# A two-block transformer part on one core: keyed sum with query and key side by side, routed weights held by TensorE, one more shared group in front

## The chip, the cores and the metric

The kernel runs on one core of one Trainium2 chip, in one launch. The metric is the device time in microseconds (us) from the start to the end of an execution; lower is better. The engines of the core are PE (TensorE), DVE (VectorE), ACT (ScalarE), POOL (GpSimd) and SP (which only issues DMAs). Each runs a program of its own and waits on semaphores for the others.

## The reference

The input is x, 2048 tokens of D = 256 features in float32, and two blocks follow. Each is `x + a(norm(x))`, `ffn`, `x + b(norm(x))`, `ffn` with its own a, b and ffn. Three functions matter here. The keyed sum (the second mixer of the first block) sees the tokens as 2 sequences of 1024:

```python
QKV = jnp.einsum('bsd,ed->bse', X, W_in) + b_in
Q, K, V = jnp.split(QKV, 3, axis=-1)
Q = rope(Q, rot_dim)
K = rope(K, rot_dim)
A = jnp.sum(feature_map(K) * V, axis=-2)
Y = A[:, None, :] * Q
Y = jnp.einsum('bsd,ed->bse', Y, W_out) + b_out
```

rot_dim is 128, with interleaved pairs; feature_map(x) is x over the larger of its norm and 1e-12; the mixer also adds its own input to Y.

The first block's ffn, once after each mixer, with 4 experts and the one best for each token:

```python
g = jnp.einsum('td,edf->tef', x, Wg)
u = jnp.einsum('td,edf->tef', x, Wu)
h = jax.nn.silu(g) * u
y = jnp.einsum('tef,efd->ted', h, Wd)
```

Each goes from 256 to 1024 features and back; only the chosen expert's row is kept, times its probability.

The second block's ffn has 8 experts of 176 hidden features, the two best for each token, and a shared expert of 352 hidden features that every token passes.

## The kernel before

The 2048 tokens lie in SBUF as NT = 16 tiles of 128 (c.x), in NG = 4 groups of 4; a sequence of the keyed sum has BT = 8 tiles, FT = 2 is the count of 128-feature halves. Every stage is a class with one method for each engine (tensor, scalar, vector, gpsimd, sync), and Core lets each engine run its methods of all stages in a row, so an engine's order of work is the order of these calls; only semaphores tie the engines together. A float32 matmul is two passes of PE and shows as two records. The stages are: attention; routed ffn (profile time about 570 to 800 us); keyed sum and its projection (828 to 920); routed ffn (to 1162); linear attention; top-two ffn (1269 to 1471); attention; top-two ffn (1805 to the end).

**Routed (L1461 to L1640).** After the tokens are sorted by expert (choose, find_starts, place_tokens, set_rows, find_owners of Routing), the stage works on 19 tiles of 128 sorted rows, each of one expert. For tile k POOL gathers its rows from DRAM (gather, L1430) and PE turns them (turn_y, L1533; the copy back is set_y on DVE). `up(k)` (L1542) multiplies them with the expert's gate and up weights, four groups of 512 columns; the tokens are the stationary operand and the weights move, at an address made from the tile's owner, which is loaded into a register (tile_owner, L1458). ACT makes silu of the gate banks (L1597), DVE multiplies with the up banks (L1630). `turn_h(k)` (L1552) transposes the result in 8 blocks, ACT copies one half back (L1602) and DVE the other (L1635). `down(k)` (L1563) multiplies with the third weight matrix, ACT evicts (out, L1592), POOL scatters to DRAM (L1434). PE's order in a step is up(k), turn_y(k + 1), down(k - 1), turn_h(k). The steps between the first and the last run in a hardware loop (Fori).

**TopTwo (L1642 to L1943).** The same with 8 experts and 39 tiles, and a shared expert for all tokens in 4 groups of 512 tokens. A group is 3 steps n: shared_up(n) (L1752) and shared_down(n) (L1763), with shared_silu on ACT, shared_mul (L1889) and shared_add (L1896) on DVE. Group 0 stands ahead of the 39 tiles, between the steps of the sort; the groups 1 to 3 stand behind them (shared_steps). Behind them too, DVE adds the routed results to x in 8 pairs of tiles (L1448) with the next norm's steps (L280 to L291); `pairs_behind` says behind which step n each pair stands.

**KeyedSum (L1946 to L2107) and Project (L347 to L433).** For each of 16 tiles PE makes q, k and v (L2022; k and v in one bank, q in another). DVE adds the bias from PSUM in three operations (L2066, L2067, L2071), and multiplies the first 128 features of q and k by cos (L2081, one each) and by sin (L2083, two each, for the interleaved pairs). POOL adds the two parts (L1992, one for q, one for k), ACT squares k and sums it (L2043), POOL takes the root of 8 tiles at once (L1997), DVE the reciprocal (L2054, L2056). `product(b)` on DVE (L2059) multiplies k by its norm's reciprocal and by v, 8 operations; it stands behind tile 9 for the first sequence and behind the loop for the second. Then PE sums over the tokens with a column of ones as the moving operand (L2031), for both sequences behind all products; DVE scales W_out by the sum (L2092); POOL adds the normed rows to x, a tile at a time in the loop (L2001, `xy`), and the bias of the projection, 16 operations behind its last root (L2009). Project turns q in 4 groups (L380), multiplies it with the scaled weights (L394), and DVE adds the result to x (L424) with the next norm, a pair of tiles at a time. `finished(pe, 0)` lets the projection start when all is rotated, and `finished(pe, 3)` waits for all scaled weights.

## Time and profile before

| | us |
|---|---|
| three runs, median (lowest to highest) | 2004.8 (2002.64 to 2005.82) |
| the profiled execution, own time | 2006.96 |
| its span, first to last instruction | 2005.2 |
| mean granted clock of TensorE, share of full speed | 0.935 |

Busy time in the span: PE 1801.9 us (90%), DVE 1121.3 (56%), ACT 755.6 (38%), POOL 555.1 (28%). PE's busy time counts matmuls alone; weight loads (1012.1 us) overlap them. A busy count includes the tail of a group of instructions, which overlaps the next group; distances between starts tell the pace. The row "x16" of a timeline is 16 instructions in a row of one line and shape. The share of a whole span says little of a stage: the stages have different limits, and each is read from its own stretch.

### The profile page before, as it was taken

The page shows a single profiled execution, that of the slowest core. Times are in us where ns is not written, and L with a number is a line of the kernel's source. Part 1 is how long each engine was busy: PE and PEld are TensorE (multiplying, and loading weights), DVE is VectorE, ACT ScalarE, POOL GpSimd, SP SyncE. Part 2 cuts the span into 40 slices and gives each one's busy share as a digit, 9 for nine tenths or more (in the row PEclk, how much of TensorE's full clock was granted, in tenths as well). Part 3 has the DMA queues.
Part 4 walks back from the last instruction along what each step waited for, and adds up shares of the span by engine and source line. Part 5 has one row for each costly group of instructions (what it writes and reads, how often), then busy time and mean ns, then how long its engine had stood idle before and what let it go on. Part 6 is the DMA issues. An engine that isn't in the chain of part 4 may idle for free.

```text
span 2005.2 us, 31961 instructions
## 1 busy us (share of the span) xinstructions
PE 1801.9 (90%) x10672; PEld 1012.1 (50%) x10673; DVE 1121.3 (56%) x2299; ACT 755.6 (38%) x1469; POOL 555.1 (28%) x954
## 2 busy tenths in 40 slices
PE   7799999999969999676999969888987999988888
PEld 4344444443346665354666636566553444455654
DVE  6688888887242221765222255733465888746334
ACT  3277777777421111112112111222132676752220
POOL 2322222222111111452111140266133222223650
PEclk9699999999689999778999989899996999998999
DMA  3311111113310000301000050122414122002223
GB/s 107 87 36 42 42 42 42 40 37 144 117 52 26 21 24 19 97 1 50 23 21 24 21 176 10 61 87 87 123 52 86 23 42 40 3 18 70 90 76 124
DMA packets 82074, 114.36 MB, mean 57 GB/s; under 512 B 17273, under 2 KB 61465, under 8 KB 81177
## 3 DMA queue, kind: packets, MB, share of 16 engines
q1 hardware_dynamic: 70808, 82.23, 14.4%
q0 software_dynamic: 11136, 30.42, 4.8%
...
## 4 chain that ended last, share of the span: by engine, by line
PE 70%; DVE 16%; issue 4%; DMA 3%; another core or an unknown queue 2%; POOL 1%; ACT 1%; SPq 0%; POOLq 0%; DVEq 0%; ACTq 0%
PE psum L1542 13%; PE psum L1064 9%; PE psum L1048 7%; DVE region_a L812 7%; PE psum L1563 7%; PE psum L1009 6%; PE psum L1781 4%; PE psum L1752 3%; PE psum L1763 2%; PE psum L1800 2%; PE psum L1552 2%; PE psum L1801 1%; PE psum L938 1%; PE psum L1033 1%
## 5 line engine op out<-in xcount | busy, mean ns | idle before, releaser
L812 DVE TENSOR_REDUCE region_a<-psum 128x1 f32<-128x640 f32 (+7 forms) x576 | 528.4, 954 | 109.1 <-PE psum L1014 57.6
L916 ACT ACTIVATE region_w<-psum 128x512 f32<-128x512 f32 x864 | 465.6, 600 | 222.7 <-PE psum L1048 219.3
L1542 PE MATMUL psum<-region_w,region_a 128*128 x608 | 271.2, 599 | 1.5 <-DVE region_a L1623 1.2
L1064 PE MATMUL psum<-region_w,region_a 128*32 128x512 f32 (+3 forms) x2304 | 253.8, 514 | 1.0 <-POOL region_w L739 0.6
L739 POOL TENSOR_SCALAR_AFFINE_SELECT region_w<-region_w 128x512 f32<-128x512 f32 x192 | 122.3, 637 | 458.7 <-ACT region_w L916 454.6
L1009 PE MATMUL psum<-region_a,y_norm 48*128 48x512 bf16 (+7 forms) x816 | 224.1, 351 | 4.9 <-DVE region_a L812 3.8
L1048 PE MATMUL psum<-y_norm,region_a 51*128 51x512 bf16 (+1 forms) x612 | 205.4, 399 | 7.0 <-DMA y_norm<-region_a 5.2
L1542 PEld LDWEIGHTS psum<-region_w,region_a 128*128 128x128 f32 x608 | 114.0, 193 | 132.2 <-issue 132.2
L1630 DVE TENSOR_TENSOR region_a<-psum,region_a 128x512 f32<-128x512 f32 x76 | 52.6, 692 | 215.1 <-PE psum L1542 215.1
L1430 POOL DMA_INDIRECT region_a<-token_rows,region_a x116 | 113.1, 975 | 147.5 <-DVE region_a L1406 86.8
L1563 PE MATMUL psum<-region_w,region_a 128*128 x608 | 137.7, 379 | 1.9 <-ACT region_a L1602 1.9
L1434 POOL DMA_INDIRECT answer_rows<-region_a x38 | 37.6, 990 | 345.5 <-ACT region_a L1592 345.5
L1048 PEld LDWEIGHTS psum<-y_norm,region_a 51*128 51x128 bf16 (+1 forms) x612 | 51.0, 96 | 161.6 <-ACT region_w L916 108.6
L1563 PEld LDWEIGHTS psum<-region_w,region_a 128*128 128x128 f32 x608 | 112.7, 190 | 17.1 <-issue 3.3
L1597 ACT ACTIVATE region_a<-psum 128x512 f32<-128x512 f32 x76 | 45.4, 597 | 187.3 <-PE psum L1542 187.3
L1012 PE MATMUL psum<-region_a 64*128 64x128 bf16 x512 | 112.5, 226 | 0.0
L1781 PE MATMUL psum<-region_w,region_a 128*128 x312 | 111.5, 482 | 0.3 <-DVE region_a L1901 0.2
L1635 DVE COPY region_a<-psum 128x512 f32<-128x512 f32 x38 | 26.3, 692 | 127.9 <-PE psum L1552 127.9
L1014 PE MATMUL psum<-region_a,identb 64*128 64x64 bf16 x512 | 97.8, 193 | 0.0
L1434 POOL DMA_INDIRECT answer_rows<-ctx,region_a x78 | 77.2, 990 | 66.8 <-ACT ctx L1861 49.1
L323 PE MATMUL psum<-identf,y_norm 128*128 128x128 f32 x256 | 44.7, 326 | 52.4 <-DVE y_norm L291 42.2
L1752 PE MATMUL psum<-y_t,region_w 128*128 128x512 f32 (+1 forms) x192 | 85.7, 594 | 0.9 <-ACT ctx L1861 0.9
...
## 6 DMA issues: line engine op xcount, KB each, us to landing
...
```

The costliest lines, as they stand in the source:

```text
L739: pool.affine_select(p, p, pattern=[[0, GQ], [1, P]], channel_multiplier=-1, base=0, compare_op=ALU.is_ge, fill=0.0)\
L812: dve.tensor_reduce(dst, src, AX_X, ALU.max, negate=True).then_inc(self.ring_done.sem, 1)
L916: act.activation(self.p[col % P_RING][:, :, i % 4, :], c.bank[ST_BANKS[s % 3]].rearrange("p (h t) -> p h t", h=GQ), ACT.Exp, scale=self.sc ...
L1009: mm = pe.matmul(bank[:, 0:n], q, kp[lo_row:hi_row, lo:lo + n], start=True, stop=not diag, skip_group_check=True)
L1048: mm = pe.matmul(bank[:, :], self.kp[slot][0:self.srows, P * j:P * j + P], self.qp[slot][0:self.srows, :, P * i:P * i + P], start=True, st ...
L1064: mm = pe.matmul(c.bank[ACC_BANK][32 * h:32 * h + 32, P * lo:512], self.vp[slot][:, j, :], self.p[col % P_RING][:, h, lo:4, :], start=(j = ...
L1430: pool.indirect_dma_start(y, None, self.c.tokens[:, :], bass.IndirectOffsetOnAxis(ap=self.row_in[:, k:k + 1], axis=0)).then_inc(done.sem, 16)
L1434: pool.indirect_dma_start(self.c.answers[0:self.spare_rows + self.top * NTOK, :], bass.IndirectOffsetOnAxis(ap=self.row_out[:, k:k + 1], a ...
L1542: mm = pe.matmul(bank[:, :], self.yt[:, f, :], w[:, f, bass.ds(own * self.hidden + 512 * half, 512)], start=(f == 0), stop=(f == FT - 1))
L1563: mm = pe.matmul(c.bank[7][:, 0:D], self.ht[:, j, :], self.wd[:, bass.ds((own * (last + 1) + j) * D, D)], start=(j == 0), stop=(j == last))
L1752: mm = pe.matmul(c.bank[6 * (n % 2) + k][0:m, :], weight[:, f, P * j:P * j + m], c.yt[:, f, 512 * g:512 * g + 512], start=(f == 0), stop=( ...
L1781: mm = pe.matmul(self.gu_bank[j][:, 0:2 * self.hidden], self.yt[j][:, f, :], w.wgu[:, f, bass.ds(owner[k] * (2 * self.hidden), 2 * self.hi ...
```

## The change

Three stages are edited.

- KeyedSum: q and k lie side by side in one buffer `qk`. PE makes q|k first (512 columns), then v (256), and each is waited for by itself. DVE adds one bias to q|k, takes cos and sin for q and k together (1 and 2 operations), and multiplies k by v, without the norm, two tiles later. POOL rotates q and k in one operation and adds the projection's bias in the loop. PE's sum takes the norm's reciprocal of each token as its moving column, in place of ones. The first sequence's sum stands behind tile 13, the second's inside the projection, ahead of its third turn. The reciprocals and the scaling of weights move with them, by `before_pair` and `finished`.
- Routed: per tile ACT copies the expert's gate weights and DVE its up weights into one of two buffers, and PE holds 128x128 blocks of these while the turned tokens move, so that h comes out transposed. turn_h and both copies of it are gone. h is double buffered, the loops are unrolled.
- TopTwo: shared group 1 stands in front of the tiles; behind them stand groups 2 and 3, with `pairs_behind` fitted to it.

Long runs of removed lines stand in the functions above.

```diff
-            own = self.tile_owner(pe, k)
             pe.wait_ge(self.y_set.sem, self.y_set.at(k + 1))
             for half in range(2):
...
+                if k:
+                    pe.wait_ge(self.h_done.sem, self.h_done.at(2 * k - 1 + half))
+                for w, copied, bank, done in ((self.gate[k % 2], self.gate_copied, c.bank[half], self.gprod),
+                                              (self.upper[k % 2], self.up_copied, c.bank[2 + half], self.uprod)):
+                    if half == 0:
+                        pe.wait_ge(copied.sem, copied.at(k + 1))
+                    for q in range(4):
+                        for f in range(FT):
+                            mm = pe.matmul(bank[:, P * q:P * q + P],
+                                           w[:, f, 512 * half + P * q:512 * half + P * q + P],
+                                           self.yt[:, f, :], start=(f == 0), stop=(f == FT - 1))
                     mm.then_inc(done.sem, 1)
 
...
+        def down(k):
+            own = owner.pop(k)
+            pe.wait_ge(self.h_done.sem, self.h_done.at(2 * k + 2))
+            if k:
                 pe.wait_ge(self.o_set.sem, self.o_set.at(k))
             last = self.hidden // P - 1
             for j in range(last + 1):
-                mm = pe.matmul(c.bank[7][:, 0:D], self.ht[:, j, :], self.wd[:, bass.ds((own * (last + 1) + j) * D, D)],
-                               start=(j == 0), stop=(j == last))
+                mm = pe.matmul(c.bank[7][:, 0:D], self.h[k % 2][:, j, :],
+                               self.wd[:, bass.ds((own * (last + 1) + j) * D, D)], start=(j == 0), stop=(j == last))
             mm.then_inc(self.down.sem, 1)
 
-        def step(k, first, last):
+        turn_y(0)
+        owner[0] = self.tile_owner(pe, 0)
+        for k in range(self.tiles):
             up(k)
-            if not last:
+            if k + 1 < self.tiles:
                 turn_y(k + 1)
...
+                owner[k + 1] = self.tile_owner(pe, k + 1)
+            if k:
+                down(k - 1)
+        down(self.tiles - 1)
...
-        def step(k, first, last):
+        def copy_gate(k):
+            own = self.tile_owner(act, k)
+            if k >= 2:
+                act.wait_ge(self.gprod.sem, self.gprod.at(2 * k - 2))
+            act.activation(self.gate[k % 2], self.wg[:, :, bass.ds(own * self.hidden, self.hidden)], ACT.Copy)\
+                .then_inc(self.gate_copied.sem, 1)
+
+        self.weights.wait(act)
+        act.wait_ge(self.owners.sem, self.owners.at(1))
+        self.places_read(act)
+        for k in range(2):
+            copy_gate(k)
+        for k in range(self.tiles):
+            if k >= 1 and k + 1 < self.tiles:
+                copy_gate(k + 1)
             for half in range(2):
                 act.wait_ge(self.gprod.sem, self.gprod.at(2 * k + half + 1))
+                if k:
+                    act.wait_ge(self.h_done.sem, self.h_done.at(2 * k - 1 + half))
                 act.activation(self.g[:, 512 * half:512 * half + 512], c.bank[half][:, :], ACT.Silu)\
                     .then_inc(self.silu.sem, 1)
...
+            if k:
+                out(k - 1)
...
+        def copy_up(k):
+            own = self.tile_owner(dve, k)
+            if k >= 2:
+                dve.wait_ge(self.uprod.sem, self.uprod.at(2 * k - 2))
+            dve.tensor_copy(self.upper[k % 2], self.wu[:, :, bass.ds(own * self.hidden, self.hidden)])\
+                .then_inc(self.up_copied.sem, 1)
+
+        self.weights.wait(dve)
+        dve.wait_ge(self.owners.sem, self.owners.at(1))
+        self.places_read(dve)
+        set_y(0)
+        for k in range(2):
+            copy_up(k)
+        for k in range(self.tiles):
+            if k >= 1 and k + 1 < self.tiles:
+                copy_up(k + 1)
+            h = self.h[k % 2].rearrange("p j t -> p (j t)")
             for half in range(2):
                 at = slice(512 * half, 512 * half + 512)
                 dve.wait_ge(self.uprod.sem, self.uprod.at(2 * k + half + 1))
                 dve.wait_ge(self.silu.sem, self.silu.at(2 * k + half + 1))
-                dve.tensor_tensor(self.h[:, at], c.bank[2 + half][:, :], self.g[:, at], ALU.mult)\
+                if k >= 2:
+                    dve.wait_ge(self.down.sem, self.down.at(k - 1))
+                dve.tensor_tensor(h[:, at], c.bank[2 + half][:, :], self.g[:, at], ALU.mult)\
                     .then_inc(self.h_done.sem, 1)
-            if not last:
+            if k + 1 < self.tiles:
                 set_y(k + 1)
...
+        shared_up(3)
         self.invert(pe, 1)
         shared_down(2)
+        shared_up(4)
+        shared_down(3)
+        shared_up(5)
+        shared_down(4)
+        shared_down(5)
         pe.wait_ge(self.owners.sem, self.owners.at(1))
-        pe.wait_ge(self.s_added.sem, self.s_added.at(2))
+        pe.wait_ge(self.s_added.sem, self.s_added.at(4))
         for k in range(2):
             turn_y(k)
             owner[k] = self.tile_owner(pe, k)
@@ -1832,7 +1850,7 @@
         self.every_tile(step)
         down(self.tiles - 1)
         pe.wait_ge(self.o_set.sem, self.o_set.at(self.tiles))
-        self.shared_steps(pe, (1, 2, 3), shared_up, shared_down, {8: 0})
+        self.shared_steps(pe, (2, 3), shared_up, shared_down, {10: 0})
...
         shared_add(0)
+        for n in range(3, 6):
+            shared_mul(n)
+        shared_add(1)
         dve.wait_ge(self.h_clear.sem, self.h_clear.at(RING))
         for k in range(2):
             set_y(k)
         mul(0)
         self.every_tile(step)
-        pairs_behind = {5: 0, 6: 1, 7: 2, 8: 3, 10: 4, 11: 5}
-        for n in range(3, 3 * NG):
+        pairs_behind = {7: 0, 8: 1, 9: 2, 10: 3, 11: 4}
+        for n in range(6, 3 * NG):
             shared_mul(n)
-            if n % 3 == 1 and n > 4:
+            if n % 3 == 1 and n > 7:
                 shared_add(n // 3 - 1)
             if n in pairs_behind:
                 self.next_norm.pair(dve, pairs_behind[n])
         shared_add(NG - 1)
-        self.next_norm.pair(dve, 6)
-        self.next_norm.pair(dve, 7)
+        for n in range(5, NT // 2):
+            self.next_norm.pair(dve, n)
...
         def rotated(t):
 
-            pool.wait_ge(self.cosm, 2 * t + 2)
-            pool.wait_ge(self.sinm, 4 * t + 4)
-            for n, z in enumerate((c.cx[:, D * t:D * t + P], self.k[:, t, 0:P])):
-                pool.tensor_tensor(z, self.ta[t % 2][:, n, :], self.tb[t % 2][:, n, :], ALU.add).then_inc(self.rot, 1)
+            pool.wait_ge(self.cosm, t + 1)
+            pool.wait_ge(self.sinm, 2 * t + 2)
+            pool.tensor_tensor(self.qk[:, t, :, 0:P], self.ta[t % 2], self.tb[t % 2], ALU.add).then_inc(self.rot, 1)
 
         def root(b):
             s = slice(b * BT, b * BT + BT)
@@ -2003,10 +2024,21 @@
                 rotated(t - 1)
             if t == BT + 1:
                 root(0)
+            pool.wait_ge(self.xy, t + 1)
+            pool.tensor_tensor(c.x[:, t, :], c.x[:, t, :], self.bias_out, ALU.add).then_inc(self.biased, 1)
         rotated(NT - 1)
         root(1)
-        for t in range(NT):
-            pool.tensor_tensor(c.x[:, t, :], c.x[:, t, :], self.bias_out, ALU.add).then_inc(self.biased, 1)
+
+    def sum_up(self, pe, b):
+
+        c = self.c
+        pe.wait_ge(self.kv, (b + 1) * BT)
+        pe.wait_ge(self.norm_step, 2 * b + 2)
+        for f in range(FT):
+            for t in range(b * BT, b * BT + BT):
+                mm = pe.matmul(c.bank[7][:, f:f + 1], c.yn[:, t, P * f:P * f + P], self.rnorm[:, t:t + 1],
+                               start=(t == b * BT), stop=(t == b * BT + BT - 1))
+        mm.then_inc(self.sums, 1)
...
-                if t >= 2:
-                    pe.wait_ge(self.lin, 2 * (t - 1))
-                    pe.wait_ge(self.v_done, t - 1)
-                for bank, lo, n in ((2 * (t % 2), D, 2 * D), (2 * (t % 2) + 1, 0, D)):
+                for i, (lo, n, free) in enumerate(((0, 2 * D, self.lin), (2 * D, D, self.v_done))):
+                    if t >= 2:
+                        pe.wait_ge(free, t - 1)
                     for f in range(FT):
...
+                        mm = pe.matmul(c.bank[2 * (t % 2) + i][:, 0:n], c.yt[:, f, P * t:P * t + P],
+                                       self.w[:, f, lo:lo + n], start=(f == 0), stop=(f == FT - 1))
+                    mm.then_inc(self.prod, 1)
+                if t == BT + 5:
+                    self.sum_up(pe, 0)
...
+    def invert_norm(self, dve, b):
+        s = slice(b * BT, b * BT + BT)
+        dve.wait_ge(self.root, b + 1)
+        dve.tensor_scalar(self.norm[:, s], self.norm[:, s], 1e-12, None, ALU.max).then_inc(self.norm_step, 1)
+        dve.wait_ge(self.norm_step, 2 * b + 1)
+        dve.reciprocal(self.rnorm[:, s], self.norm[:, s]).then_inc(self.norm_step, 1)
+
+    def scale_weights(self, dve, b):
+        dve.wait_ge(self.sums, b + 1)
+        for f in range(FT):
+            dve.tensor_scalar(self.ws[b][:, f, :], self.wo[:, f, :], self.c.bank[7][:, f:f + 1], None,
+                              ALU.mult).then_inc(self.scaled, 1)
...
+        def key_value(t):
+            dve.wait_ge(self.rot, t + 1)
+            dve.wait_ge(self.v_done, t + 1)
+            dve.tensor_tensor(c.yn[:, t, :], c.yn[:, t, :], self.qk[:, t, 1, :], ALU.mult).then_inc(self.kv, 1)
 
         for t in range(NT):
-            kv, q = c.bank[2 * (t % 2)], c.bank[2 * (t % 2) + 1]
+            qk, v = c.bank[2 * (t % 2)], c.bank[2 * (t % 2) + 1]
             bt = t % BT
-            dve.wait_ge(self.prod, t + 1)
-            dve.tensor_tensor(cx[:, t, :], q[:, 0:D], self.bias[:, 0:D], ALU.add).then_inc(self.lin, 1)
-            dve.tensor_tensor(self.k[:, t, :], kv[:, 0:D], self.bias[:, D:2 * D], ALU.add).then_inc(self.lin, 1)
-
+            dve.wait_ge(self.prod, 2 * t + 1)
+            dve.tensor_tensor(self.qk[:, t, :, :].rearrange("p n d -> p (n d)"), qk[:, :], self.bias[:, 0:2 * D],
+                              ALU.add).then_inc(self.lin, 1)
+
+            dve.wait_ge(self.prod, 2 * t + 2)
             dve.wait_ge(self.xy, t + 1)
             self.ln.ready(dve, t // 4)
-            dve.tensor_tensor(c.yn[:, t, :], kv[:, D:2 * D], self.bias[:, 2 * D:3 * D], ALU.add).then_inc(self.v_done, 1)
-
-            dve.wait_ge(self.lin, 2 * t + 2)
+            dve.tensor_tensor(c.yn[:, t, :], v[:, 0:D], self.bias[:, 2 * D:3 * D], ALU.add).then_inc(self.v_done, 1)
+
+            dve.wait_ge(self.lin, t + 1)
             if t >= 2:
-                dve.wait_ge(self.rot, 2 * t - 2)
-            a, b = self.ta[t % 2], self.tb[t % 2]
+                dve.wait_ge(self.rot, t - 1)
+            a, b, z = self.ta[t % 2], self.tb[t % 2], self.qk[:, t, :, 0:P]
             sin = self.sin[:, bt, :].rearrange("p (n e) -> p n e", e=2)
...
+            dve.tensor_tensor(a, z, over(self.cos[:, bt, :], 1, 2), ALU.mult).then_inc(self.cosm, 1)
+            pair, bp = (y.rearrange("p m (n e) -> p m n e", e=2) for y in (z, b))
+            for e in range(2):
+                dve.tensor_tensor(bp[:, :, :, e], pair[:, :, :, 1 - e], over(sin[:, :, e], 1, 2), ALU.mult)\
+                    .then_inc(self.sinm, 1)
+            if t >= 2:
+                key_value(t - 2)
+            if t == BT + 3:
+                self.invert_norm(dve, 0)
+        key_value(NT - 2)
+        key_value(NT - 1)
+        self.scale_weights(dve, 0)
+
+    def before_pair(self, dve, n):
+        if n == 0:
+            self.invert_norm(dve, 1)
+            dve.wait_ge(self.biased, NT)
+        if n == 2:
+            self.scale_weights(dve, 1)
 
     def source(self, t, f):
-        return self.c.cx[:, D * t + P * f:D * t + P * f + P]
+        return self.qk[:, t, 0, P * f:P * f + P]
 
     def out_weights(self, t, f):
         return self.ws[t // BT][:, f, :]
 
     def finished(self, pe, g):
-        if g == 0:
-            pe.wait_ge(self.rot, 2 * NT)
+        pe.wait_ge(self.rot, 4 * g + 4)
+        if g == 1:
+            pe.wait_ge(self.scaled, FT)
+        if g == 2:
+            pe.wait_ge(self.project.ot1, (NG - 1) * self.project.k + 1)
+            self.sum_up(pe, 1)
+        if g == 3:
             pe.wait_ge(self.scaled, NB * FT)
```

## Rows read from the trace of the kernel before

**Rows 1.** The page's part 4: the chain that ended last, by engine.

```profile
PE 70%; DVE 16%; issue 4%; DMA 3%; another core or an unknown queue 2%; POOL 1%; ACT 1%; SPq 0%; POOLq 0%; DVEq 0%; ACTq 0%
```

**Rows 2.** Table by stretches: first routed and keyed-sum stage; busy us (instructions).

```profile
578.90:799.90 221.00, 219.63 (x796) 135.14 (x796) 45.42 (x75) 40.52 (x76) 35.07 (x36) 0.99 0.07 21
827.80:920.20 92.40, 76.61 (x314) 55.73 (x312) 68.80 (x234) 15.71 (x46) 48.04 (x84) 0.87 0.01 2
```

**Rows 3.** Timeline of PE, one routed tile: start, us, line, operands, count.

```profile
669.65 7.03 PE L1542 MATMUL psum<-region_w,region_a 128*128 x16
...
676.74 3.62 PE L1563 MATMUL psum<-region_w,region_a 128*128 x16
680.20 1.04 PE L1552 MATMUL psum<-identf,region_a 128*128 128x128 f32 x8
681.07 7.03 PE L1542 MATMUL psum<-region_w,region_a 128*128 x16
```

**Rows 4.** Timeline of PE, linear attention: 129-column passes with own weights.

```profile
1225.79 7.31 PE L2211 MATMUL psum<-region_w,region_a 128*128 128x129 f32 x64
```

**Rows 5.** Timeline of PE, the keyed sum's two sums by a one-column matmul.

```profile
874.80 3.63 PE L2031 MATMUL psum<-region_a 128*128 128x1 f32 x32
888.06 6.99 PE L2031 MATMUL psum<-region_a 128*128 128x1 f32 x32 [9.63 <-DVE region_a L2059]
```

**Rows 6.** Timeline of PE, the end of the first routed stage.

```profile
796.13 3.71 PE L1563 MATMUL psum<-region_w,region_a 128*128 x16 [0.95 <-ACT region_a L1602]
```

**Rows 7.** Groups of instructions by shape: evictions of the routed stages; busy, mean ns.

```profile
L1630 DVE TENSOR_TENSOR region_a<-psum,region_a 128x512 f32<-128x512 f32 x76 | 52.6, 692 | 215.1 <-PE psum L1542 215.1
...
L1597 ACT ACTIVATE region_a<-psum 128x512 f32<-128x512 f32 x76 | 45.4, 597 | 187.3 <-PE psum L1542 187.3
...
L1592 ACT ACTIVATE region_a<-psum 128x256 f32<-128x256 f32 x38 | 14.6, 384 | 183.9 <-PE psum L1563 183.9
```

**Rows 8.** Timeline of POOL in the same tile: gather of the next rows.

```profile
671.02 0.97 POOL L1430 DMA_INDIRECT region_a<-token_rows,region_a  x1 [0.30 <-issue]
```

**Rows 9.** Timeline of DVE in the keyed-sum loop, second half.

```profile
866.32 0.88 DVE L2083 TENSOR_TENSOR region_a<-ctx,region_a 128x64 f32<-128x64 f32 x2
...
868.79 0.88 DVE L2083 TENSOR_TENSOR region_a<-ctx,region_a 128x64 f32<-128x64 f32 x2
...
876.68 0.36 DVE L2083 TENSOR_TENSOR region_a<-region_a 128x64 f32<-128x64 f32 x2
```

**Rows 10.** Timeline of POOL beside it: the add of the normed rows (xy).

```profile
866.18 0.80 POOL L2001 TENSOR_TENSOR x_res<-x_res,y_norm 128x256 f32<-128x256 f32 x1
```

**Rows 11.** Timeline of DVE: the second half's products, then two pairs of the projection.

```profile
881.31 6.70 DVE L2059 SCALAR_TENSOR_TENSOR region_a<-region_a,y_norm 128x256 f32<-128x256 f32 x8
...
907.93 0.75 DVE L424 TENSOR_TENSOR x_res<-psum,x_res 128x256 f32<-128x256 f32 x2
...
910.09 0.75 DVE L424 TENSOR_TENSOR x_res<-psum,x_res 128x256 f32<-128x256 f32 x2
```

**Rows 12.** Timeline of PE: two steps of the shared expert behind the tiles.

```profile
1424.70 1.89 PE L1763 MATMUL psum<-region_w,ctx 128*128 128x256 f32 x8
...
1429.86 1.89 PE L1763 MATMUL psum<-region_w,ctx 128*128 128x256 f32 x8
```

**Rows 13.** Timeline of DVE behind the last shared add: two pairs with their norm.

```profile
1463.13 0.87 DVE L1448 SCALAR_TENSOR_TENSOR x_res<-y_norm,region_a,x_res 128x256 f32<-128x256 f32 x2
...
1466.20 0.88 DVE L1448 SCALAR_TENSOR_TENSOR x_res<-y_norm,region_a,x_res 128x256 f32<-128x256 f32 x2
```

**Rows 14.** Timeline of PE ahead of the first top-two tiles.

```profile
1287.74 0.39 PE L1396 MATMUL psum<-region_a 128*128 128x117 bf16 x4 [1.80 <-DVE region_a L1379]
...
1295.07 1.47 PE L1774 MATMUL psum<-identf,region_a 128*128 128x128 f32 x4 [1.43 <-DVE x_res L1896]
1296.64 2.71 PE L1781 MATMUL psum<-region_w,region_a 128*128 x4
...
1301.27 1.35 PE L1781 MATMUL psum<-region_w,region_a 128*128 x4
```

143 lines of the change are left out of this document (32 added, 111 removed).

## The prediction

> **What bounds the kernel now.** I read the chain of work that ended last first: TensorE (PE) carries 70% of it, VectorE (DVE) 16% [rows 1]. So most of the change is judged by PE's time. The table by stretches then shows the two kinds of stage that it touches: in a routed stage PE is busy for 219.63 of 221.00 us at a granted clock of 0.99, so nothing but fewer PE microseconds helps there; in the keyed-sum stage PE is busy for 76.61 of 92.40 us and DVE for 68.80, at 0.87, so there the order of the steps decides [rows 2]. Last come the timelines of single engines for the terms of the sum. Run-to-run differences here allow about 0.2% (4 us) to be told from no change.
>
> **Routed stages (two, 19 tiles each).** One tile is 11.42 us, from one start of L1542 to the next (681.07 - 669.65). L1542 takes 6.86 of it as 16 passes of 512 columns (0.429 each), with turn_y (0.22) to L1563's start at 676.74; down (L1563) takes 3.46 to 680.20; the turns of h (L1552, 8 passes) take 0.87 [rows 3]. The change makes the up step 32 matmuls, so 64 passes of 128 columns, each with its own weight load, and drops the turns. The nearest row is another stage's: 64 passes of 129 columns with weights of their own in 7.31 us, so 0.1117 apart (7.31 less the last pass's tail, 64 ways) [rows 4]. A second row agrees: 32 passes of one column in 3.63 [rows 5]; the price is the weight load and not the columns. Up becomes 64 x 0.1117 = 7.15, 0.29 more; the turns give 0.87 back. The static addresses and the single expert load a tile change only what PE's queue issues, and 1.4 us in 221 is all the idleness there is, so I count nothing. New tile: 7.15 + 0.22 + 3.45 = 10.82, 0.60 less; for 17 intervals 10.2 us.
> At the stage's end PE now turns h (1.0), waits 0.95 for the copy of it and does the last down [rows 6]; turns and wait both go, 2.0. Against it, down(18) must wait for out(17) to free the only bank, about 0.65 by the 0.38 of such an eviction [rows 7] and a hand-over. At the start the first passes run at the lower clock, where 128-column passes cost no more than the four times longer ones relative to full speed: nothing. Per stage 10.2 + 2.0 - 0.65 = 11.5, twice is 23.0.
> What must stay covered: ScalarE (ACT) copies 2048 columns of gate weights a tile, DVE as many up weights. By the 512-column eviction, 0.597 (ACT) and 0.692 (DVE) [rows 7], four such are 2.4 and 2.8; by the slope between the 256- and 512-column evictions ACT needs 1.9. Either lies in a tile in which each engine has over 6 us free (45 us of DVE and 41 of ACT work in 221, of which the h copies go) [rows 2]. POOL issues the row gather at 671.02, 1.4 us after L1542 started [rows 8]; the up step that hides it and its landing gets no shorter. If a copy delayed a tile, the price would be the delay past some 2 us of slack, 38 times. Bounds for the two stages together: 17 (each tile 0.15 dearer) to 26.
> The Trainium skill ("SBUF — State Buffer", the warning box "The 'DVE blocks DMA' trap (SWDGE)") speaks against this part: an fp32 SBUF-to-SBUF copy on DVE locks GpSimd out of the shared port, so that it can't write a gather's descriptors. If it did so for the whole copy each tile, the gather would come 2 to 3 us later, within about 2 us of slack: at worst 1 us a tile, 38 us in all. Copy and gather stand in no row together here.
>
> **Keyed sum and its projection.** PE needs 4 passes each of 512 and 256 columns a tile, 4 x 0.429 x 1.5 = 2.57 us [rows 3]. DVE's tile lasts 2.47 in the second half, from one L2083 pair of 0.88 to the next (868.79 - 866.32), of which 0.52 is a wait for POOL's add at 866.18 (0.80), since the last pair, without one, takes 0.36; so 1.95 [rows 9, 10]. The new tile has one 512-column add for two of 256, two sine products for four and one product k*v of 256 columns: about 2.0 alone. POOL now does its rotation as one operation and the bias add (L2009) inside the loop, so three of DVE's operations meet POOL's. Bounds of a tile: 2.58, where PE sets it, and 3.45, where each SBUF operation of DVE waits for one of POOL's 0.80; I take 2.8, since one wait of 0.52 a tile is the rule now [rows 9] and I expect one to two. Reading starts earlier by 1.5, as DVE waits for 8 passes of half clock and not 12 (first copy at 831.3). 16 x 2.8 = 44.8 from there, plus 1 for sum_up(0), which holds PE for 3.6, and 0.8 for the reciprocal gives 877 to 878; two products and two scalings of 0.3 more, 880.
> Before, the tail after the loop (877.04) was: root and reciprocal to 881.31, eight products 6.70, PE's second sum at the lower clock 6.99 from 888.06 after an idle 9.63, then scaling and turns before the first product [rows 5, 11]. Now the norm rides as the moving column, so the 6.70 stands in the loop; and sum_up(1) comes inside the projection, while PE is warm. New: turn(1) waits for the scaled weights, 880 to 881; multiply(0) to 884.7; sum_up(1) 3.6 to 888.3 (32 passes at 0.1117 [rows 5]); turn(2) and multiply(1) to 892.7, whose first pair is read at about 891.2; six pairs at 2.16 (910.09 - 907.93) [rows 11] follow, ending at about 905 with the last norm against 920.2 [rows 2]. invert_norm(1) and its wait for the bias adds stand in DVE ahead of pair 0: behind them are queued all adds of the projection, so root(1) on POOL (1.65) is hidden only because multiply(0) takes 3.5. **Saved: 15.2**, by the tile's bounds 8 to 18.
>
> **Front groups of the top-two stages.** A step of a shared group (up and down) takes 5.16, from one down to the next (1429.86 - 1424.70) [rows 12], so a group is 3 x 5.16 = 15.5 of PE. Moving one to the front takes 15.5 from behind, but one more pair (5, 6, 7, not 6, 7) now follows the last add: 3.07 with norm (1466.20 - 1463.13) [rows 13], so the back of the first such stage saves 12.4; in the last stage a pair is only its two L1448 groups, 1.6, and the gain 13.9. In front PE idles 1.8 us before the second inversion and 1.4 before turn_y(0) [rows 14]; the new steps fill only the first, since turn_y still waits for an add. turn_y(0) comes at about 1305.6 for 1295.07, 10.6 later: 15.5 less the hole filled, less 3 us of DVE's work on rows and owners that now runs under PE's steps. The third product of group 1 is queued on DVE behind that work and shared_add(0), so down(3) may wait some 0.5; I leave that in the bounds. After it L1781's first four passes took 2.71 [rows 14], twice the 1.35 of those from 1301.27 on; with PE kept busy ahead the clock is up already, and of the 4 us between 2.0 come back. Front cost 8.6; net 3.8 and 5.3, together 9.0. Bounds 5 (no clock gain) to 13 (the inversion's wait goes whole).
>
> **The sum.** 23.0 + 15.2 + 9.0 = 47.2 us. The profiled execution lasted 2006.96 us, so 1959.8; it stood 2.2 above the median of the runs, 2004.8, so **1958** on the median.
>
> **Rivals.** (A) DVE and POOL alternate in every operation of the keyed-sum loop: 3.45 a tile, 16 x 0.65 = 10.4 more, 1968. For it: L2059 beside POOL's adds took 0.84 each (6.70 for 8) [rows 11], as long as an add of POOL. Against: only one pair of four meets one in rows 9. The Trainium skill ("SBUF — State Buffer", section "SBUF: two separate sides") states that one of the pair takes the port for the whole instruction and the other fully blocks; by that every meeting costs up to 0.8, and it leans to A. By that the trace agrees: 0.52 was lost under an add that ran on for 0.66 [rows 9, 10].
> (B) The front groups don't fill holes and the clock doesn't rise earlier: 5 us less gain, 1962 to 1963.
> (C) The other side, **slower**: the 128-column passes with own weights run at the lower clock. [rows 5] hold both levels for weight-bound passes: 32 in 3.63 at 2.4 GHz and 32 in 6.99 at 1.2 GHz. The up step would be 64 x 0.214 = 13.7, 6.5 more than with the clock up; over 38 tiles 247 us, so 2205, and 2300 if turn_y and down are slowed with it (3.67 more a tile, less what overlaps). Its turning point: the other parts save 24.2, the tiles 0.60 x 38 = 22.8; over 64 x 38 = 2432 passes 47.0 is 0.019, so from a mean pass of 0.131 on the kernel is slower. Against it: the 64 passes of 129 columns in rows 4 ran at full speed and followed a full-clock stretch; for it: they lasted only 7 us, and no row shows such a mix for 200 us.
> (D) It doesn't do what it says: the copies or the gather come late, 1 us a tile, 38 less, 1996.
>
> **Chances.** Forecast (1950 to 1964, with B in it) 0.61; A 0.18; better than it, up to 1945, 0.05; D 0.07, a seventh of it near no change; C 0.04 and slower by something not seen here 0.03; no change from several small losses 0.02. The range, 1943 to 1982, holds forecast, A and half of D. Faster by over 0.2%: 0.61 + 0.18 + 0.05 + 0.06 = 0.90; within it 0.01 + 0.02 = 0.03; slower 0.07.
>
> **What would show it.** L1542's successor as x64 in about 7.3 us and a period of 10.8 with no idle before it; no L1552; granted clock 0.99 in the routed stretches. DVE's tile in the keyed sum at 2.8, and the projection's pairs ending near 905 after the earlier shift of 11.5. sum_up(1) in 3.6 and not 7. L1781's first four passes in 1.4 after turn_y(0). Wrong would be: idle before turn_y or before up in each tile (D), passes of 0.2 (C), a POOL add under every DVE operation (A), a first pair that waits for POOL's root.

## The result

The changed kernel took 1968.8 us (median of 4 runs, 1968.63 to 1969.58) against 2003.7 for the kernel before in the same rounds (4 runs, 2002.1 to 2005.82): a ratio of 0.9816, with a 95% interval of 0.9804 to 0.9829. The forecast was 1958. The profiled executions were 1968.63 and 2006.96 us, 38.3 apart where the sum said 47.2.

The profile after, first its busy times and the chain by engine (before: [rows 1]); PE is the bound as it was:

```profile
PE 1776.6 (90%) x12192; PEld 1134.3 (58%) x12192; DVE 1134.2 (58%) x2235; ACT 802.7 (41%) x1469; POOL 553.6 (28%) x937
...
PE 71%; DVE 15%; issue 4%; DMA 3%; another core or an unknown queue 2%; POOL 2%; ACT 1%; SPq 0%; POOLq 0%; DVEq 0%; ACTq 0%
```

The table by stretches (before: [rows 2]); the columns are stretch, its length, busy us and instructions of PE, PEld, DVE, ACT and POOL, granted clock, DMA share, GB/s. Both routed stages and the keyed sum:

```profile
581.80:791.40 209.60, 207.83 (x1556) 199.05 (x1556) 55.06 (x76) 61.66 (x75) 35.06 (x36) 0.99 0.07 24
819.40:901.70 82.30, 76.72 (x316) 53.59 (x317) 63.89 (x170) 15.45 (x46) 45.69 (x67) 0.91 0.01 2
921.90:1132.10 210.20, 208.52 (x1556) 199.68 (x1556) 54.98 (x75) 61.52 (x74) 35.01 (x36) 0.99 0.07 24
```

The first routed stage lasts 209.6 for 221.0, the keyed sum 82.3 for 92.4 to 92.8. PEld is nearly as busy as PE now in the routed stages (199.05 for 207.83 us, 135.14 before): each pass has its own weight load.

Where the time went, from PE's first instruction of each stretch to that of the next (us); a routed stretch ends with its last down, and the last stretch with DVE's last add. "Other traces" are those of the experiments below whose code in the stretch is that of the changed kernel (for a stretch that no edit touches, all of them):

| stretch | before | after | difference | other traces |
|---|---|---|---|---|
| start to the first router (no edit) | 559.57 | 562.42 | +2.85 | 557.7 to 565.7 |
| routed, first | 220.86 | 209.41 | -11.45 | 209.2 to 209.7 |
| keyed sum and projection | 92.79 | 82.30 | -10.49 | 79.0 to 83.4 |
| routed, second | 220.59 | 210.10 | -10.49 | 209.1 to 210.7 |
| top-two 1: front | 27.20 | 37.67 | +10.47 | 37.5 to 37.7 |
| top-two 1: tiles | 117.65 | 118.64 | +0.99 | 116.5 to 120.4 |
| top-two 1: behind | 57.38 | 44.98 | -12.40 | 44.98 to 44.99 |
| top-two 2: front | 27.33 | 37.53 | +10.20 | 37.5 |
| top-two 2: tiles | 117.47 | 114.04 | -3.43 | 115.3 to 121.2 |
| top-two 2: behind | 51.21 | 37.31 | -13.90 | 37.31 |
| all other stretches up to that add (no edit) | 509.85 | 509.14 | -0.71 | |

The routed tile in the trace after (PE; start, us, line, operands; before: [rows 3]), and the end of the stage (before: [rows 6]):

```profile
667.94 7.31 PE L1549 MATMUL psum<-region_a,ctx 128*128 128x128 f32 x64
675.09 0.38 PE L1533 MATMUL psum<-identf,region_a 128*128 128x128 f32 x2
675.30 3.62 PE L1561 MATMUL psum<-region_w,region_a 128*128 x16
678.76 5.41 PE L1549 MATMUL psum<-region_a,y_norm 128*128 128x128 f32 x47
```

```profile
783.27 3.62 PE L1561 MATMUL psum<-region_w,region_a 128*128 x16
787.57 3.72 PE L1561 MATMUL psum<-region_w,region_a 128*128 x16 [0.69 <-ACT region_a L1585]
```

678.76 - 667.94 is 10.82, and 16 of the stage's 18 intervals are 10.82; the first two are 10.23 and 10.92. The 64 passes take 7.31 as those of [rows 4] did. At the end the last down waits 0.69 for the eviction of the one before.

The weights' copies, on DVE and then on ACT, and what POOL issues in that tile (before: [rows 8]):

```profile
665.46 1.23 DVE L1629 COPY y_norm<-region_w 128x2048 f32 x1
```

```profile
668.79 1.91 ACT L1591 ACTIVATE y_norm<-region_w 128x2048 f32 x1 [0.27 <-issue]
```

```profile
668.80 0.99 POOL L1437 DMA_INDIRECT answer_rows<-region_a  x1 [8.55 <-ACT region_a L1585]
670.10 0.97 POOL L1433 DMA_INDIRECT region_a<-token_rows,region_a  x1 [0.30 <-issue]
```

DVE's 2048 columns take 1.23 us, not the 2.8 that I had from four PSUM evictions; ACT's take 1.91, as the slope said. DVE's copy is over at 666.7, POOL's first issue starts at 668.8: they never meet.

The keyed-sum loop on DVE, one tile of the second half (before: [rows 9]):

```profile
843.10 0.68 DVE L2096 TENSOR_TENSOR region_a<-psum,region_a 128x512 f32<-128x512 f32 x1
843.70 0.41 DVE L2102 TENSOR_TENSOR y_norm<-psum,region_a 128x256 f32<-128x256 f32 x1
844.03 0.70 DVE L2109 TENSOR_TENSOR region_a<-region_a,ctx 128x256 f32<-128x256 f32 x1
844.66 1.01 DVE L2112 TENSOR_TENSOR ctx<-region_a,ctx 128x128 f32<-128x128 f32 x2
845.59 0.41 DVE L2090 TENSOR_TENSOR y_norm<-y_norm,region_a 128x256 f32<-128x256 f32 x1
845.93 0.68 DVE L2096 TENSOR_TENSOR region_a<-psum,region_a 128x512 f32<-128x512 f32 x1
```

845.93 - 843.10 is 2.83. L2109 (cosines, 0.70) and L2112 (sines, 1.01 for two) each hold one wait for POOL, since they take 0.41 and 0.48 where POOL is idle. But the end of the loop and the start of the projection hold something that isn't in the forecast. PE's timeline there, and its granted clock (the first of the last three numbers of a row) in slices of 2 us:

```profile
858.99 4.26 PE L2039 MATMUL psum<-region_a,y_norm 128*128 128x1 f32 x32 [0.32 <-DVE region_a L2075]
863.11 8.21 PE L2053 MATMUL psum<-region_a,y_t 128*128 128x512 f32 x16
871.16 1.04 PE L382 MATMUL psum<-identf,region_a 128*128 128x128 f32 x8
874.74 1.12 PE L382 MATMUL psum<-identf,region_a 128*128 128x128 f32 x8 [2.54 <-DVE ctx L2080]
875.66 5.29 PE L396 MATMUL psum<-ctx,y_t 128*128 128x256 f32 x16
880.78 3.63 PE L2039 MATMUL psum<-region_a,y_norm 128*128 128x1 f32 x32
```

```profile
859.00:861.00 2.00, 2.00 (x19) 2.00 (x19) 2.00 (x7) 0.12 (x2) 1.17 (x3) 1.00 0.00 0
861.00:863.00 2.00, 2.00 (x16) 2.00 (x15) 2.00 (x4) 0.51 (x2) 2.00 (x3) 0.74 0.00 0
863.00:865.00 2.00, 2.00 (x5) 0.97 (x5) 0.80 (x3) 0.51 (x2) 1.50 (x3) 0.50 0.00 0
865.00:867.00 2.00, 2.00 (x4) 0.97 (x3) 0.09 (x1) 0.00 (x0) 0.75 (x2) 0.50 0.00 0
867.00:869.00 2.00, 2.00 (x5) 1.35 (x5) 0.98 (x3) 0.00 (x0) 0.00 (x0) 0.55 0.00 0
869.00:871.00 2.00, 2.00 (x8) 1.19 (x7) 1.61 (x6) 0.27 (x1) 1.07 (x2) 1.00 0.00 0
...
877.00:879.00 2.00, 2.00 (x6) 1.63 (x5) 0.42 (x1) 0.00 (x0) 0.00 (x0) 0.50 0.00 0
```

L2039 is the first sum, 32 passes of one column: it starts at the full clock, and 3 us into it the clock falls to 1.2 GHz, while PE is busy in 100% of the slice. The 16 passes behind it, the two last tiles of the loop, end at 871.3, 8.1 after the sum, where two tiles at full clock are 2 x 2.57; DVE waits for them. A second low stretch follows PE's 2.54 us of idle time at 872 to 874.7: multiply(0) (L396) takes 5.12 to the next start (880.78 - 875.66) where later ones take 3.45.

### The profile page after: what moved, and what is told of

Its sections match the earlier page's. It is cut to its first block, busy times and chain, and to the rows that moved or that the text cites. A ratio compares the mean times of both kernels' runs of the same rounds, so it can differ in the third digit from the quotient of the medians.

```text
span 1966.9 us, 34312 instructions
## 1 busy us (share of the span) xinstructions
PE 1776.6 (90%) x12192; PEld 1134.3 (58%) x12192; DVE 1134.2 (58%) x2235; ACT 802.7 (41%) x1469; POOL 553.6 (28%) x937
## 4 chain that ended last, share of the span: by engine, by line
PE 71%; DVE 15%; issue 4%; DMA 3%; another core or an unknown queue 2%; POOL 2%; ACT 1%; SPq 0%; POOLq 0%; DVEq 0%; ACTq 0%
PE psum L1549 14%; PE psum L1067 9%; PE psum L1051 8%; DVE region_a L815 7%; PE psum L1561 7%; PE psum L1012 6%; PE psum L1764 4%; PE psum L1793 4%; PE psum L1775 2%; PE psum L1812 2%; PE psum L1813 1%; PE psum L941 1%; PE psum L2240 1%; PE psum L1036 1%
## 5 line engine op out<-in xcount | busy, mean ns | idle before, releaser
L1012 PE MATMUL psum<-region_a,y_norm 48*128 48x512 bf16 (+7 forms) x816 | 228.2, 356 | 4.9 <-DVE region_a L815 4.2
L1549 PEld LDWEIGHTS psum<-region_a,ctx 128*128 128x128 f32 x1280 | 149.9, 196 | 3.0 <-DVE region_a L1623 2.0
L1549 PE MATMUL psum<-region_a,ctx 128*128 128x128 f32 x1280 | 150.4, 280 | 1.2 <-DVE region_a L1623 1.2
L1561 PE MATMUL psum<-region_w,region_a 128*128 x608 | 137.8, 380 | 1.4 <-ACT region_a L1585 1.4
L1549 PE MATMUL psum<-region_a,y_norm 128*128 128x128 f32 x1152 | 131.7, 275 | 1.8 <-DVE region_a L1623 1.8
L1549 PEld LDWEIGHTS psum<-region_a,y_norm 128*128 128x128 f32 x1152 | 131.3, 192 | 3.1 <-DVE region_a L1623 2.3
L1561 PEld LDWEIGHTS psum<-region_w,region_a 128*128 128x128 f32 x608 | 112.5, 190 | 16.0 <-issue 2.2
L1793 PE MATMUL psum<-region_w,region_a 128*128 x312 | 109.0, 473 | 0.7 <-issue 0.7
L1012 PEld LDWEIGHTS psum<-region_a,y_norm 48*128 48x128 bf16 (+1 forms) x816 | 66.2, 100 | 41.4 <-DVE region_a L815 21.3
```

The costliest lines, as they stand in the source:

```text
L1012: mm = pe.matmul(bank[:, 0:n], q, kp[lo_row:hi_row, lo:lo + n], start=True, stop=not diag, skip_group_check=True)
L1549: mm = pe.matmul(bank[:, P * q:P * q + P], w[:, f, 512 * half + P * q:512 * half + P * q + P], self.yt[:, f, :], start=(f == 0), stop=(f = ...
L1561: mm = pe.matmul(c.bank[7][:, 0:D], self.h[k % 2][:, j, :], self.wd[:, bass.ds((own * (last + 1) + j) * D, D)], start=(j == 0), stop=(j == ...
L1793: mm = pe.matmul(self.gu_bank[j][:, 0:2 * self.hidden], self.yt[j][:, f, :], w.wgu[:, f, bass.ds(owner[k] * (2 * self.hidden), 2 * self.hi ...
```

## The experiments

Each is timed against the kernel before in the same rounds. The chips differed (the kernel before had medians of 2011.4, 2008.7 and 2006.5 us on the three), so ratios are compared, or stretches of traces.

### One part alone, three times

The kernel before with the classes of one stage taken from the changed kernel: routed_only has Routed, keyed_only has KeyedSum with the hooks in Stage and Project, top_only has TopTwo.

> The kernel before with the edit of the routed stages alone. Theory: the edit's worth is the shorter tile, 10.82 us for 11.42, and the shorter end, 11.4 us a stage in the trace of the full change, so the time is about 22 us under the kernel before, ratio 0.989, and the first routed stage starts within 1 us of where it did (579.0). Rival, that the longer program (loops written out) costs elsewhere: the first routed stage starts 2.8 us later, as it did with all three edits, though no line ahead of it is changed; then the gain is 19 to 20.

> The kernel before with the edit of the keyed sum and its projection alone. Theory: it gives the 10.5 us that this stage gave within the full change, ratio 0.9948, and both falls of TensorE's granted clock show again: one in the 32 one-column passes of the sum inside the loop, one in the first product of the projection. Rival, that these falls were chance: one or both are missing, the stage takes 82.3 - 3.3 or - 1.7 us, and the gain is 12 to 15.

> The kernel before with the edit of the top-two stages alone. Theory: the backs save 12.4 and 13.9 us and the fronts cost 10.5 each, as in the full change, so 5 to 6 us net before what the clock does at the first tiles; with it (low there in the first stage and full in the second of the full change) 4 to 9, ratio 0.9955 to 0.998. Rival, that the forecast was right with 9.0: ratio 0.9955 with a full clock at the first tile of both stages.

Measured: routed_only 0.9928 (0.9906 to 0.9950), keyed_only 0.9939 (0.9915 to 0.9963), top_only 0.9952 (0.9935 to 0.9969). The three losses of time, 0.72, 0.61 and 0.48%, add to 1.81%; the whole change has 1.84%. So the parts are additive within what the timing resolves (0.17 to 0.24% each). routed_only's stages last 209.33 and 209.71; its first router starts at 558.25, earlier than in the kernel before, so the rival of a longer program that costs elsewhere is out: the +2.85 ahead of every edit is no part of the change (that stretch ran from 557.7 to 565.7 us in the traces shown here). The timed gain of routed_only, 15.6 us between the medians, is under the 22 that I expected, and the expected ratio of 0.989 lies outside the interval; its two stages have their 22.4, but the old keyed sum in that trace took 96.4 for 92.8 (after the 3.33 us in which PE waits for DVE's products, 32 passes took 13.33 for 10.56, so a low clock there), and the untouched tiles of the top-two stages took 120.2 and 121.8 for 117.6 and 117.5. keyed_only gave 9.4 us in its stretch (83.38) and shows both falls of the clock, and a third of 3.4 us further on. top_only has the fronts at 37.49 twice and the backs at 44.98 and 37.31.

### wide_sum and sum32: how many columns the sum moves

```diff
-                mm = pe.matmul(c.bank[7][:, f:f + 1], c.yn[:, t, P * f:P * f + P], self.rnorm[:, t:t + 1],
+                mm = pe.matmul(c.bank[7][:, P * f:P * f + P], c.yn[:, t, P * f:P * f + P],
+                               self.rnorm[:, t:t + 1].to_broadcast([P, P]),
...
-            dve.tensor_scalar(self.ws[b][:, f, :], self.wo[:, f, :], self.c.bank[7][:, f:f + 1], None,
+            dve.tensor_scalar(self.ws[b][:, f, :], self.wo[:, f, :], self.c.bank[7][:, P * f:P * f + 1], None,
```

sum32 is the same with 32 columns for 128.

> The changed kernel, but the sums' moving operand is the norm's reciprocal repeated over 128 columns, for 1 column; the results stand 128 times and one of them is read. Theory: a pass costs its weight load, 0.112 us, at 1 column as at 128, but with one column TensorE's granted clock falls during the sum in the loop (from 861.9 to 869.0) and costs 3.3 us; with 128 columns the clock stays up, the sum takes 3.6 for 4.3, the products behind it 2.57 a tile, and the kernel is 3.3 us faster than the changed kernel (about 1965.5). Rival, that the fall comes from the short idle times ahead of the sum (0.25 and 0.32 us) or by chance: it is there again and the time is 1968.8.

> The changed kernel with the reciprocal repeated over 32 columns as the sums' moving operand. [...]

PE in wide_sum, then its granted clock in the same stretch; below them PE in sum32:

```profile
856.90 3.81 PE L2039 MATMUL psum<-region_a,y_norm 128*128 128x128 f32 x32 [0.32 <-DVE region_a L2076]
860.54 5.32 PE L2054 MATMUL psum<-region_a,y_t 128*128 128x512 f32 x16
```

```profile
859.50:861.50 2.00, 2.00 (x14) 1.52 (x14) 2.00 (x5) 0.51 (x2) 1.51 (x2) 1.00 0.00 0
861.50:863.50 2.00, 2.00 (x8) 1.24 (x7) 1.06 (x3) 0.51 (x2) 2.00 (x3) 1.00 0.00 0
```

```profile
857.09 4.22 PE L2039 MATMUL psum<-region_a,y_norm 128*128 128x32 f32 x32 [0.32 <-DVE region_a L2076]
861.13 8.30 PE L2054 MATMUL psum<-region_a,y_t 128*128 128x512 f32 x16
```

With 128 columns the sum ends 3.64 after its start and the two tiles behind it take 5.17; the clock is 1.00 through both (the fall at multiply(0) stays: 5.10 to the next start). With 32 columns it is as with one: the sum 4.04, the tiles 8.1. From the sum's start to the loop's last pass:

| traces | columns | us |
|---|---|---|
| after, keyed_only, early_scale, late_copy, early_copy | 1 | 12.31 to 12.34 |
| no_bias_add | 1 | 12.24 |
| after_again, early_turn | 1 | 10.66, 10.67 |
| sum32 | 32 | 12.34 |
| wide_sum, all_four | 128 | 8.98, 8.97 |

All nine with 1 or 32 columns lose 1.7 or 3.4 us, none of the two with 128 does. In after_again and early_turn the fall begins later, behind the sum (6.93 for the two tiles), and their loops had come there 1.6 us earlier; so they lose less. The whole stage would not have shown the effect: 78.95 in wide_sum, 82.36 in sum32, but also 79.00 in after_again with one column, because there the clock rose 1.9 us after the stage's first pass, for 5.1 and 5.2 in wide_sum and sum32. The ratio of wide_sum, 0.9787 (0.9760 to 0.9815), isn't told apart from the changed kernel's 0.9816, nor the expected gain from the rival's none: 3.3 us is less than the other stretches vary.

### early_scale, early_copy: PE's wait ahead of the projection

early_scale moves the scaling of the first sequence's weights ahead of the last products; early_copy also moves the copies of the turned q ahead of DVE's last product and ACT's last square. The edit of early_copy, shortened; early_scale has only its lines with scale_weights:

```diff
             if t == BT + 3:
                 self.invert_norm(dve, 0)
+            if t == NT - 2:
+                self.scale_weights(dve, 0)
         key_value(NT - 2)
+        self.project.first_copy(dve)
         key_value(NT - 1)
-        self.scale_weights(dve, 0)
...
         for t in range(NT):
+            if t == NT - 1:
+                self.project.copy_turned(act, 0)
             act.wait_ge(self.rot, t + 1)
```

> The changed kernel with the scaling of the first sequence's weights moved on DVE from behind the loop's last two products to behind tile 14's steps, so that the projection's second turn finds it done. Theory: TensorE's 2.54 us of idle time ahead of that turn goes, and with it the fall of the granted clock from 875 to 879 that makes the first product 5.1 for 3.45: the keyed-sum stage takes 82.3 - 2.5 - 1.7, about 78.5 us by its stretch; the first fall, in the sum inside the loop, stays. Rival: the projection then waits for something else of the same length (the second reciprocal, whose root ends on POOL at 875.8, or the rotation), and the stage gains under 1 us.

> The changed kernel with the weights of the first sequence scaled behind tile 14, and the projection's first two copies of the turned q placed ahead of DVE's last product and ahead of ACT's last square. early_scale took away the wait for the scaled weights, and a wait for these copies of the same length came in its place (2.63 us). Theory: with both gone TensorE goes from its turns to the first product with under 1 us idle, the product takes 3.5 for 4.9, and the keyed-sum stage about 78.5 by its stretch. Rival: the second sum, which needs the root and the reciprocal of the second half (876.3 in the changed kernel's trace), waits instead and takes the gain back.

PE in early_scale, then in early_copy:

```profile
866.90 1.91 PE L382 MATMUL psum<-identf,region_a 128*128 128x128 f32 x16
871.44 5.23 PE L396 MATMUL psum<-ctx,y_t 128*128 128x256 f32 x16 [2.63 <-DVE y_t L420]
```

```profile
870.42 1.91 PE L382 MATMUL psum<-identf,region_a 128*128 128x128 f32 x16
874.39 5.38 PE L396 MATMUL psum<-ctx,y_t 128*128 128x256 f32 x16 [2.06 <-ACT y_t L418]
```

Both theories missed, and in early_scale the rival came true in kind: a wait of the same length, and 0.2 us gained. The second turn runs through (x16), but the wait comes back ahead of the first product, 2.63 and then 2.06 us, and the product behind it is slow as before (5.07 and 5.22 to the next start). The stretches are 82.06 and 81.94 for 82.30; the ratios 0.9812 (0.9793 to 0.9832) and 0.9805 (0.9780 to 0.9829). DVE works without a gap through the steps of tile 15 up to that copy (in early_copy from 868.15 to 873.57): it is DVE's queue that PE waits for. The row of early_copy names ACT, but ACT's copy for that product was over at 871.66; DVE's ended at 874.25, 0.14 before PE started, and in early_scale at 871.30, 0.14 before it too. What is left is to put the copy ahead of tile 15's own rotation; that wasn't tried.

### no_bias_add: one POOL operation fewer in each tile

The adds of the projection's bias on POOL and the wait for them are left out, so the output lacks that bias.

> The changed kernel without the adds of the projection's bias on POOL (left out altogether, so the output lacks that bias). Theory: the tile of 2.83 us in the keyed-sum loop is 2.58 of TensorE's own plus what DVE's sine and cosine steps wait for POOL; with two of POOL's operations a tile for three, one wait of 0.3 to 0.5 goes and the tile falls to TensorE's 2.58, so the stage gains 16 x 0.25 = 4 us. Rival, that the two-engine waits come from the rotation and the add of the normed rows alone: the tile stays at 2.8.

DVE, two starts of one line in the loop:

```profile
841.06 0.69 DVE L2094 TENSOR_TENSOR region_a<-psum,region_a 128x512 f32<-128x512 f32 x1 [0.22 <-PE psum L2051]
...
843.64 0.69 DVE L2094 TENSOR_TENSOR region_a<-psum,region_a 128x512 f32<-128x512 f32 x1 [0.22 <-PE psum L2051]
```

The tile is 2.58, PE's own pace, and the first sum starts 2.6 us earlier in the stage (37.0 for 39.6 after its first pass). So the waits for POOL that PE's pace doesn't hide were 0.25 of a tile. The stage took 81.29, only 1.0 less where 4 were expected: the first product took 4.6 to the next start, and a low clock in multiply(1) made it 5.14 for 3.45. The ratio is 0.9806 (0.9786 to 0.9826).

### late_copy: DVE's copy beside POOL's issue

```diff
             if k >= 1 and k + 1 < self.tiles:
+                if k >= 2:
+                    dve.wait_ge(self.o_set.sem, self.o_set.at(k - 1))
                 copy_up(k + 1)
```

> The changed kernel, but in the routed stages DVE starts its copy of 2048 columns only when the result of the tile before last is evicted, so that it runs at the same time as POOL's issue of the scatter (now 0.99 us) and ahead of the gather's. Theory from the trace of the change, where copy and issue never meet: there is some 2 us of slack, so the tile stays at 10.82 whatever the copy does to the issue. The rule of the Trainium skill (SBUF — State Buffer, the box on DVE blocking DMA) says that POOL can't write descriptors during the copy: the scatter's issue then takes 1.5 to 2.2 us for 0.99 and the gather's starts later by the same. Rival: they don't disturb each other, 0.99 and 0.97 as before.

POOL, then DVE:

```profile
664.57 1.86 POOL L1437 DMA_INDIRECT answer_rows<-region_a  x1 [7.69 <-ACT region_a L1585]
666.74 0.97 POOL L1433 DMA_INDIRECT region_a<-token_rows,region_a  x1 [0.30 <-issue]
```

```profile
665.08 1.23 DVE L1629 COPY y_norm<-region_w 128x2048 f32 x1 [3.83 <-ACT region_a L1585]
```

The scatter's issue takes 1.86 for 0.99 and ends 0.12 behind the copy. Of the 38 scatters 32 meet a copy: each takes 1.85 to 1.87 and ends 0.12 behind it, though it had started 0.5 us before it; the six that meet none take 0.97 to 0.99. The gather's own issue, behind it, stays at 0.97 and starts as much later. This agrees with the rule of the Trainium skill (SBUF — State Buffer, the box on DVE blocking DMA) that GpSimd can't write a DMA's descriptors while such a copy runs. It costs next to nothing here: of the intervals between tiles that are 10.82 in the trace after, one is 11.27 and the others stay, and the ratio is 0.9817 (0.9796 to 0.9839). The slack was there as forecast.

### early_turn: no wait for the add ahead of the tiles

```diff
+        turn_y(0)
+        owner[0] = self.tile_owner(pe, 0)
         shared_down(5)
-        pe.wait_ge(self.s_added.sem, self.s_added.at(4))
-        for k in range(2):
-            turn_y(k)
-            owner[k] = self.tile_owner(pe, k)
+        turn_y(1)
+        owner[1] = self.tile_owner(pe, 1)
         up(0)
```

The wait for the add stands ahead of turn_h(0), and DVE copies both turned tiles ahead of that add.

> The changed kernel, but in the top-two stages the turns of the first two routed tiles stand on TensorE ahead of and behind the last shared product of the front group, and the wait for the shared add stands ahead of the first use of its bank. Theory: the 3.2 us between the end of that product and the first routed product (1.43, 0.43 and 0.35 of them idle) fall to 0.5, the front takes about 34.8 for 37.5 in both stages, and the clock can't fall there: 5 us less in all. Rival: the rows' gather or DVE's copy is late instead and the front takes 37 or more.

First the changed kernel's two fronts (PE), then early_turn's first:

```profile
1270.97 3.62 PE L1775 MATMUL psum<-region_w,ctx 128*128 128x256 f32 x16
1276.02 0.41 PE L1786 MATMUL psum<-identf,region_a 128*128 128x128 f32 x2 [1.43 <-issue]
1276.85 0.43 PE L1786 MATMUL psum<-identf,region_a 128*128 128x128 f32 x2 [0.43 <-issue]
1277.64 2.01 PE L1793 MATMUL psum<-region_w,region_a 128*128 x4 [0.35 <-issue]
```

```profile
1810.72 0.41 PE L1786 MATMUL psum<-identf,region_a 128*128 128x128 f32 x2 [1.43 <-issue]
1811.38 0.43 PE L1786 MATMUL psum<-identf,region_a 128*128 128x128 f32 x2 [0.26 <-issue]
1812.19 1.45 PE L1793 MATMUL psum<-region_w,region_a 128*128 x4 [0.37 <-issue]
```

```profile
1267.72 0.38 PE L1786 MATMUL psum<-identf,region_a 128*128 128x128 f32 x2
1267.94 1.89 PE L1775 MATMUL psum<-region_w,ctx 96*128 96x256 f32 x8
1269.66 0.38 PE L1786 MATMUL psum<-identf,region_a 128*128 128x128 f32 x2
1269.89 1.35 PE L1793 MATMUL psum<-region_w,region_a 128*128 x4
```

Both fronts of the changed kernel have three waits, of 1.43, 0.43 or 0.26, and 0.35 or 0.37. In the first, the four passes of L1793 then take 2.01 and the next ones 2.31; in the second 1.45 and 1.35. So the gain that the forecast took from a warm clock came once in two here, and less often elsewhere: in the nine traces with the changed front the clock is at 1.2 GHz within the first four passes of L1793 in 14 of 18 stages (in all nine first ones). With early_turn there is no wait, both fronts take 34.90 and both first products run at full clock, as they do in all_four: no low clock there in 4 of 4. The ratio is 0.9772 (0.9738 to 0.9806). The tiles behind the front took 117.8 us on average in the 18 stretches of nine traces with the changed front, 119.4 in the six with the old one and 115.7 in the four with the early turns. Single stretches vary from 114.0 to 121.8, so the first of these differences is about what was forecast (2.0) but rests on the mean. The granted clock goes the same way: 12.0, 8.5 and 6.8 us of such a stretch lie at the lower level on average (old front, changed front, early turns), and of them 3.5, 2.4 and 0 in its first 8 us.

### after_again and all_four

after_again is the changed kernel on the chip of the last runs; all_four has wide_sum, early_scale, early_copy and early_turn in it.

> The changed kernel itself, as a control on the chip of the next runs. Theory: ratio 0.981 to the kernel before, TensorE's clock falls in the keyed sum's inner sum again (seven traces of seven with the one-column operand), and the stages without an edit differ from other traces by up to some us, so that single runs can't show gains of 3 us in the whole time.

> The changed kernel with all four edits: the sums over 128 columns, the early scaling, the early copies, and the early turns in the top-two stages. Theory: the gains add, 3.3 + 4 in the keyed sum and 5.2 in the two fronts, some 12 us less than the changed kernel on the same chip; ratio to the kernel before about 0.975. Rival, that gains of the keyed sum overlap (the clock falls once anyway): 8 us less.

In after_again the clock fell again, but behind the sum and not in it (table above). The ratios: after_again 0.9802 (0.9778 to 0.9826), all_four 0.9760 (0.9737 to 0.9783): medians 1966.5 and 1958.2 us on one chip, 8.3 apart where 12 were expected. The two fronts give 5.35 of it by their stretches. In the keyed sum all_four takes 78.67 for 82.30 of after, but 79.00 in after_again, whose loop came to the higher clock sooner. The profiled executions are 12.0 apart, as expected, but by luck: 3.4 of it lie ahead of the first router, where no edit is, and 3.2 in the top-two tiles. The early copies gave next to nothing there as well. all_four is faster than the kernel before, and its slowest run (1961.9) is under the fastest of after_again (1965.0).

## Why the prediction was right or wrong

**Direction and size.** A gain of 46.8 us on the median was forecast and 34.9 came; on the profiled executions 47.2 and 38.3. Of these 8.9 us, 6.7 lie in the edited stages (1.1 routed, 4.7 keyed sum, 0.9 top-two) and 2.1 in stretches that no edit touches: 2.85 more ahead of the first router, where routed_only shows chance, and 0.71 less elsewhere.

**Routed stages: right.** The term was 64 passes at 0.1117 from another stage's row; the tile came out at 10.82 as summed. The end's term (2.0 less 0.65) holds: the wait is 0.69. 11.45 and 10.49 came for 11.5 each; the second stage is 0.7 longer, 0.6 of it in its first two intervals, where the clock rose later (4.9 us into the stage for 3.6). The copies are hidden, DVE's at less than half the price that I gave it. The rival of thin passes at 1.2 GHz is out for 128 columns: the granted clock is 0.99 over the whole stage. It isn't out for thinner ones, and that is what the next step missed.

**Keyed sum: the mechanism right, the price of PE's part mis-sized.** DVE's tile was put at 2.8 and is 2.83, the first copy at 1.5 us earlier and is 1.25, the pairs of the projection at 2.16 and are. The step that failed is "plus 1 for sum_up(0), which holds PE for 3.6", and "multiply(0) to 884.7", taken at the full clock. I had the rows: in [rows 5] the same 32 passes took 3.63 in front of an idle stretch, so nothing behind them could show a fall. The fall in the sum costs 3.4 us (12.34 for 8.98 by wide_sum), and multiply(0) after 2.5 us of idle time takes 1.7 more (5.12 for 3.45). Together that is 5.1, of which 4.7 show between 15.2 and 10.5. The first is shown by an edit that takes it away; the second isn't, since early_scale and early_copy didn't remove the idle time, and it rests on where the low slices stand.

**Front groups: fronts and backs right, the clock term uncertain.** Fronts 10.47 and 10.20 for 10.6, backs 12.40 and 13.90 for 12.4 and 13.9. The term "2.0 come back" for a warm clock came as a loss of 1.0 in the first stage and a gain of 3.4 in the second; by the mean over traces it is 1.6. That the sum came near here (net 8.1 for 9.0) is partly luck: the term was to come from the first products, and the low clock in the first 8 us went only from 3.5 to 2.4 us, worth 0.6. I hadn't seen that turn_y's wait for the add, which I named, stands just ahead of them: with the waits the clock fell there in 14 of 18 stages, without them in none of 4. Which of the waits does it, no run separates.

**Rivals.** A (3.45 a tile) is out, the tile is 2.83; the time of 1968 that it gave was met for another reason. The meetings of the two engines show in the 0.70 and 1.01 of DVE's rows, but PE's pace hides most of them: no_bias_add gives 0.25 a tile. B is half right: in one stage of two here, and in 14 of 18 over the traces, the first products met the low clock. D is out, at least up to a late copy of 1.23 us. C is out.

**What stays open.** The sum was run with 1, 32 and 128 columns and with no other width, and the 128-column passes were seen for 200 us, the others for 4. Why the fall comes within the sum in seven traces and behind it in two isn't settled. That the idle time ahead of multiply(0) lowers its clock is argued, not shown.
